# Selective scan on one core: GpSimd multiplies the scan results of two pairs by C in one instruction, and the first transfers of layer 2 go in another order

## What is computed

```python
def step(h, inp):
    x_t, dt_t, B_t, C_t = inp
    dA = jnp.exp(dt_t[:, :, None] * A)
    h = h * dA + (dt_t * x_t)[:, :, None] * B_t[:, None, :]
    y = jnp.einsum('bdn,bn->bd', h, C_t)
    return (h, y)
...
return ys.transpose(1, 0, 2) + x * D
```

## Time and profile before

| what | value |
|---|---|
| median of 3 runs | 19420.55 us (19398.34 to 19422.17) |
| profiled execution, its own time | 19405.06 us |
| its span from first to last instruction | 19403.3 us |
| VectorE busy | 17217.6 us (89%) |
| GpSimd busy | 16892.6 us (87%) |
| TensorE matmul busy | 15381.8 us (79%) |
| ScalarE busy | 13163.4 us (68%) |
| mean granted TensorE clock | 0.879 of full speed |
| DMA, mean rate | 94 GB/s |

### The profile page before, as it was taken

How to read it: one execution, slowest core, us unless ns; L and a number is a source line. 1 busy time by engine, 2 the same in 40 slices (tenths; PEclk the granted TensorE clock), 3 DMA queues, 4 the chain that set the end, 5 groups by cost and what they waited for, 6 DMA issues and landing times. The chain is left out here.

```text
span 19403.3 us, 188542 instructions
## 1 busy us (share of the span) xinstructions
PE 15381.8 (79%) x45152; PEld 5366.5 (28%) x45152; DVE 17217.6 (89%) x13583; ACT 13163.4 (68%) x33157; POOL 16892.6 (87%) x11028
## 2 busy tenths in 40 slices
PE   7887878878788787877878778787787877878778
PEld 2222222222222222222222222222222222222222
DVE  7988979889798897989979899798997989979899
ACT  5766767667676776767767677676776767767677
POOL 6979979799797997979979799797997979979799
PEclk8888888888898888888889888888888888888888
DMA  2424424244242442424424244242442424424244
GB/s 68 122 60 111 117 60 122 58 111 117 62 119 61 109 116 65 116 65 108 112 67 118 64 109 109 67 116 66 109 110 67 118 64 111 108 67 118 64 112 108
DMA packets 880283, 1820.18 MB, mean 94 GB/s; under 512 B 189530, under 2 KB 594804, under 8 KB 879028
## 3 DMA queue, kind: packets, MB, share of 16 engines
q1 hardware_dynamic: 879028, 1806.77, 37.0%
HBM read 1083.46 MB, written 245.63 MB: 68 GB/s over the span
## 5 line engine op out<-in xcount | busy, mean ns | idle before, releaser
L1156 DVE TENSOR_TENSOR_SCAN arena<-ps,arena 128x897 f32<-128x897 f32 x5376 | 10986.1, 2064 | 762.4 <-POOL arena L1351 292.7
L1359 POOL TENSOR_TENSOR arena<-arena 128x896 f32<-128x896 f32 x5376 | 9405.3, 1766 | 279.5 <-DVE arena L1156 259.6
L1290 ACT ACTIVATE ps<-arena,A 128x448 f32<-128x448 f32 x10752 | 6391.4, 627 | 2637.9 <-DVE arena L1156 2541.8
L1062 PE MATMUL ps<-arena,rep 128*64 128x448 f32 x21504 | 5477.2, 639 | 1626.5 <-POOL arena L1359 1618.2
L1351 POOL TENSOR_TENSOR arena<-arena 128x896 f32<-128x896 f32 x2688 | 4760.1, 1771 | 385.1 <-DMA arena<-arena 385.0
L1062 PEld LDWEIGHTS ps<-arena,rep 128*64 128x64 f32 x21504 | 1477.7, 153 | 5248.9 <-POOL arena L1359 2855.0
L1145 DVE TENSOR_TENSOR arena<-ps,arena 128x896 f32<-128x896 f32 x2688 | 2862.8, 1065 | 70.8 <-PE ps L982 60.0
L1015 PE MATMUL ps<-arena,diag 128*128 128x448 f32 x5248 | 2192.7, 562 | 75.4 <-DVE arena L1119 75.4
L1054 PE MATMUL ps<-arena,skipd 128*128 128x448 f32 x1344 | 802.6, 684 | 709.9 <-DVE arena L1132 590.0
L1015 PEld LDWEIGHTS ps<-arena,diag 128*128 128x128 f32 x5248 | 986.3, 195 | 1265.2 <-issue 1045.1
L1027 PE MATMUL ps<-arena,wdt 13*128 13x448 f32 x1344 | 764.9, 676 | 508.5 <-DVE arena L1125 496.9
(11 more groups left out here) (171 smaller groups left out, 18902.2 us busy)
## 6 DMA issues: line engine op xcount, KB each, us to landing
arena<-bc_rows SPq DMA_DIRECT2D x3584, 224.0 KB, 4.6
arena<-arena SPq DMA_DIRECT2D x4160, 112.0 KB, 3.2
x_projected<-arena SPq DMA_DIRECT2D x112, 672.0 KB, 3.6
y_forward<-arena SPq DMA_DIRECT2D x112, 672.0 KB, 5.3
arena<-x_projected SPq DMA_DIRECT2D x112, 672.0 KB, 4.8
arena<-y_forward SPq DMA_DIRECT2D x112, 672.0 KB, 6.2
x<-in_x SPq DMA_DIRECT2D x119, 336.0 KB, 3.6
x_normed<-arena SPq DMA_DIRECT2D x112, 336.0 KB, 5.2
```

The lines of the kernel that those rows point to most:

```text
L1062: m = e.matmul(ps[64 * h:64 * h + 64, YBANK, 0:T], rep[:, 0:64], pr[:, (q - 1 + h) % NPR, a * T:a * T + T], start=False, stop=p == NP - 1 ...
L1156: e.tensor_tensor_scan(rev(hh[:, q % NH, 0:W2], s), rev(decays(q)[:, 0:W2], s), rev(bb[:, q % NB, 0:W2], s), car[:, 2 * k + p % 2, n:n + 1 ...
L1290: e.activation(two(decays(q))[:, a, :], dt2[:, r % NR2, p % 2, :], ACT.Exp, scale=Am[s][:, 2 * k + p % 2, n:n + 1]).then_inc(c_ex, 1)
L1359: e.tensor_tensor(pr[:, q % NPR, :].rearrange("p (a b) -> p a b", a=2), two(hh[:, q % NH, :]), cr[:, p - p % 2:p - p % 2 + 2, :], ALU.mult ...
```

## The change

Three things are done together.

1. `output(q)` becomes `outputs(q)`: one GpSimd instruction of 1792 elements a partition handles pairs q and q+1. It waits for the scan of q+1 and for the sums of the two pairs that held its places in `pr`. `hh` gets 6 places.
2. GpSimd makes its product for pair g + 3 in step g, not g + 2, and `bb` gets 4 places.
3. The transfers of dt are split into two jobs (`dd`, `de`) with a semaphore each, so that a pair waits for the half that it reads. In the first pass of an image `ud` comes between the two, and the loads of B and C alternate. In later passes `ud` is due 0.6 steps earlier.

```diff
-NB, NH, NPR = 3, 3, 4
+NB, NH, NPR = 4, 6, 4
...
-        sp.extend([(max(t + 3.4, NP * (EJ * i + e - 2) - 0.5 if i else t), "dd", i, e), (t + 5, "ud", i, e)])
+        o = max(t + 3.4, NP * (EJ * i + e - 2) - 0.5 if i else t)
+        sp.extend([(o, "dd", i, e), (o + 0.02, "de", i, e), (t + 4.4 if i or e else o + 0.01, "ud", i, e)])
...
-            sp.append((max(r + 1, t + 2 + 4 * (G > 0 and not i)), "bl", i, G))
-            sp.append((max(r + 3, t + 2.1 + 4 * (not i)), "cl", i, G))
+            if i:
+                sp.extend([(max(r + 1, t + 2), "bl", i, G), (max(r + 3, t + 2.1), "cl", i, G)])
+            else:
+                sp.extend([(t + (5.3 if G else 2) + G, "bl", i, G), (t + 5.9 + G, "cl", i, G)])
...
         def decay(q):
             r, i, k, p, s = pair(q)
-            spread(w, s_dt, 4, r)
+            spread(w, s_dt, 2 * (r % NR2) + p % 2, r)
...
-        def output(q):
+        def outputs(q):
             r, i, k, p, s = pair(q)
-            w.wait_ge(c_sc, q + 1)
+            w.wait_ge(c_sc, q + 2)
             w.wait_ge(s_cl[p // 2], 32 * (i + 1))
-            w.wait_ge(c_sm, q - NPR + 1)
-            e.tensor_tensor(pr[:, q % NPR, :].rearrange("p (a b) -> p a b", a=2), two(hh[:, q % NH, :]),
-                            cr[:, p - p % 2:p - p % 2 + 2, :], ALU.mult).then_inc(c_mc, 1)
+            w.wait_ge(c_sm, q - NPR + 2)
+            o, h = pr[:, q % NPR:q % NPR + 2, :], hh[:, q % NH:q % NH + 2, :]
+            e.tensor_tensor(o.rearrange("p h (a b) -> p h a b", a=2),
+                            h.rearrange("p h (a b) -> p h a b", a=2)[:, :, :, 0:T],
+                            cr[:, p:p + 2, :].unsqueeze(1).to_broadcast([128, 2, 2, T]), ALU.mult).then_inc(c_mc, 2)
...
-        for g in range(-AHEAD, Q + 1):
-            if g >= 1:
-                output(g - 1)
-            if g + AHEAD < Q and not ON_VECTOR[(g + AHEAD) // NP % EJ][(g + AHEAD) % NP]:
-                product(g + AHEAD)
+        for g in range(-AHEAD - 1, Q + 1):
+            if g >= 2 and g % 2 == 0:
+                outputs(g - 2)
+            if g + AHEAD + 1 < Q and not ON_VECTOR[(g + AHEAD + 1) // NP % EJ][(g + AHEAD + 1) % NP]:
+                product(g + AHEAD + 1)
             side(g)
```

More of the change, by code:

```diff
@@ L905, in build @@
     s_xl, s_nl, s_yl = ([sem(f"{k}{b}") for b in range(2)] for k in ("xp_loaded", "n_loaded", "y_loaded"))
-    s_dt, s_du = ([sem(f"{k}{b}") for b in range(NR2)] for k in ("dt_spread", "du_spread"))
+    s_dt, s_du = ([sem(f"{k}{b}") for b in range(n)] for k, n in (("dt_spread", 2 * NR2), ("du_spread", NR2)))
     s_bl, s_cl = ([sem(f"{k}{G}") for G in range(4)] for k in ("b_loaded", "c_loaded"))
@@ L941, in b_loaded, with spread @@
         w.wait_ge(s_bl[p // 2], 32 * (i + 1))
-    def spread(w, sems, parts, r):
+    def spread(w, sems, k, r):
         if r >= 0:
-            w.wait_ge(sems[r % NR2], 16 * parts * (r // NR2 + 1))
+            w.wait_ge(sems[k], 32 * (r // NR2 + 1))
     def product_done(w, q):
@@ L1240, in side @@
                     o = ps[:, bank_of("t", i, k), 0:T]
-                    spread(w, s_dt, 4, r - NDT)
+                    for h in range(2):
+                        spread(w, s_dt, 2 * ((r - NDT) % NR2) + h, r - NDT)
                     w.wait_ge(c_du, r - NDT + 1)
@@ L1338, in side @@
                     w.wait_ge(c_dp, r - NDU + 1)
-                    spread(w, s_du, 2, r - NDU)
+                    spread(w, s_du, (r - NDU) % NR2, r - NDU)
                     e.tensor_tensor(du[:, r % NDU, :], dt[:, r % NDT, :], xc[:, r % NXC, :],
@@ L1347, in product @@
             r, i, k, p, s = pair(q)
-            spread(w, s_du, 2, r)
+            spread(w, s_du, r % NR2, r)
             b_loaded(w, i, p)
@@ L1420, in layer1_sync @@
                                     [64, 2, T])).then_inc(s_cl[k], 16)
-            if name == "dd":
+            if name in ("dd", "de"):
                 r = EJ * i + k
+                h = int(name == "de")
                 freed(w, "t", i, k)
                 w.wait_ge(c_ex, 2 * NP * (r - NR2 + 1))
-                for h in range(2):
-                    for j in range(2):
-                        e.dma_start(dt2[64 * j:64 * j + 64, r % NR2, h, :],
-                                    dt[64 * h:64 * h + 64, r % NDT, :]).then_inc(s_dt[r % NR2], 16)
+                for j in range(2):
+                    e.dma_start(dt2[64 * j:64 * j + 64, r % NR2, h, :],
+                                dt[64 * h:64 * h + 64, r % NDT, :]).then_inc(s_dt[2 * (r % NR2) + h], 16)
             if name == "ud":
```

## The result

The changed kernel takes 19911.17 us (19868.46 to 19934.89, 4 runs), the kernel before 19411.45 us beside it. The ratio is **1.0255**, 95% interval 1.0236 to 1.0274: 500 us slower, far outside the predicted range, on the side that had 9% of the chances. The profiled execution took 19868.46 us.

A forecast was written before the change was run, and what follows sets the result against it. VectorE's work plus its round trips over ScalarE and TensorE was taken as the bound, not GpSimd. Per image -15.7 + 2 + 4 + 1 - 3 = -11.7 us, times 16 images -187 us: 19225 us, range 18990 to 19325.

The forecast's parts named there:

- the side that had 9% of the chances: Whole kernel: slower than before by over 0.2%, given a chance of 0.09.
- The start, -15.7 +2 us an image: Start of layer 2: earlier dt x transfers bring the first scan 15.7 us forward; late first outputs give back 2 us.
- The merged instruction, 3.3 us: GpSimd's outputs: one merged instruction takes 3.3 us where two took 3.44, saving 24 us an image on GpSimd.
- Rival 1: Steady passes: GpSimd is the bound and the merge's saving is passed on, -33 us an image, 18890 us; chance 0.2.
- I count none of it: Steady passes: none of GpSimd's 24 us an image saved shortens the path, since VectorE does not wait for GpSimd.
- The second pass, +4 us: Second pass of an image: outputs 20, 21 and a dt x follow pair 24's late product, so scan 27 comes later.
- That order stays as it was: Second pass of an image: the queue's order is kept, so pair 24's product starts as late as before in its chain.
- places worth -3 us: Steady passes: more places in `hh` and `bb` and the earlier product remove VectorE's waits for GpSimd, -3 us an image.
- I count 0 for it, with 0.8 us a pass as the upper bound: Ends of groups: sums of y up to 1.6 us later behind merged outputs cost 0, at most 0.8 us a pass.
- The range: Whole kernel: -6 to -27 us an image, 18990 to 19325 us.
- -6 us an image: The range's slow end: start giving 13 us, second pass taking 5, steady passes taking 6; 19325 us.
- Rival 3: First chunk and group ends: late outputs hold ScalarE and TensorE, 0.8 us a pass, giving back the start; 19410 us; chance 0.1.

The follow-up runs named there:

- e1_start: The kernel before with only the third part of the change at the start (order of first transfers, half-dt semaphores), later `ud` as before; 19169.25 us, ratio 0.9867.
- e2_two: The changed kernel with each merged output written as two instructions, both behind the wait for the second scan; 20015.09 us, ratio 1.0304.
- e7_places: e1_start with four places in `bb` and six in `hh`, instruction order and single outputs as before; 19171.33 us, ratio 0.9877.
- e13_two_single: e3 with single outputs for pairs 10, 11 and 18, 19 of each forward pass, all others merged; 19402.19 us, ratio 0.9995.
- e18_start_norm_first: e1_start with the norm's matmul L992 ahead of the sum of pairs 18, 19 in TensorE's order; 19112.97 us, ratio 0.9852.
- e4_single: The changed kernel with one output instruction a pair again, each after its own scan; products stay a pair further ahead; 19518.28 us, ratio 1.0053.
- e3: The changed kernel with merged outputs, but products only as far ahead as in the kernel before; 19526.62 us, ratio 1.0052.
- e8: The changed kernel with only the first product of each group of pairs a step later, behind the next merged output; 19642.79 us, ratio 1.012.
- e10: e3 with six places for products with C and four for scan results; 19467.76 us, ratio 1.0019.
- e14: e3 with single outputs everywhere except pairs 10, 11 and 18, 19 of each forward pass, which stay merged; 19340.8 us, ratio 0.9968.
- e15: e3 with L1025 and L992 ahead of the sums of pairs 10, 11 and 18, 19 in TensorE's order; 19526.66 us, ratio 1.0065.
- e17: e3 with only L992 ahead of the sum of pairs 18, 19 in TensorE's order; 19460.67 us, ratio 1.0025.
- e11_backward: e3 with merged outputs in the backward passes alone, single ones in the forward passes; 19252.15 us, ratio 0.9909.
- e16_start_jobs_first: e1_start with L1025 and L992 ahead of the sums of pairs 10, 11 and 18, 19 in TensorE's order; 19442.32 us, ratio 1.0018.
- e9_lag_room: e3 with TensorE's sums one pair later, six places for products with C and four for scan results; 19961.44 us, ratio 1.0265.

## Why the prediction was wrong

- **The start, -15.7 +2 us an image.** Right within 1.3 us in the rows shown, and e1_start measured 16 us.
- **The merged instruction, 3.3 us.** Right, 3.31. Rival 1 fell: GpSimd was the busiest engine of a pass, but e2_two, which has 360 us more work on it than the changed kernel, is only 104 us (half a point) slower, where rival 1 needed the whole saving of 390 us to be passed on, 2 points. "I count none of it" was a little too strict. The Trainium skill says to optimise the engine with the highest occupancy first (Perfetto Trace Analysis, section Identifying the Most-Contended Engine); here that was GpSimd, and relieving it gave back under a third of its saved time.
- **The second pass, +4 us.** The delay came as worked out (16.0 us against 16.1), but its price did not: the lead lengthens the first two passes by 9.6 us with single outputs, and by 7.6 us with merged ones. How the delay grows on its way is not shown.
- **"That order stays as it was", and places worth -3 us.** This step failed. Places alone gave nothing (e7_places). The prediction priced the earlier product at the one pass where the trace of before already showed a wait for dt x. In the seven later passes where that wait was hidden by GpSimd's own work, with 1.2 us to spare in the pass shown, the lead took this cover away. Measured: 1.76 points, 21 us an image, where the sum had -3 + 4. Nearly half of it stands in the first two passes, the other half mostly in the passes with the new wait.
- **"I count 0 for it, with 0.8 us a pass as the upper bound".** This step failed by size. The 1.6 us of lateness was right and measured as 1.65. Its argument, that the convolution holds the sums anyway, was read at the ends of groups; what TensorE's order holds behind a sum in the middle of a group (L1025, L992) was not looked at. Measured: 1.85 points, 22 us an image, by the traces some 3.6 us in each of the four forward passes from the third on, and by the times 0.7 in a backward one.
- **The range.** Its slow end, -6 us an image, is not what its own bounds add up to: -13 + 2 + 5 + 1 + 6 is +1 us, about 19440 us. The result lies far above that too.
- **Rival 3** was this mechanism, at 0.8 us a pass and with a chance of 0.1. It should have had a bound of the full 1.6 us for each sum with something behind it, plus the slower matmuls.

The sum with measured terms: start -258, lead +340, merge +359 us, together +440 us of 500 measured. The remaining 60 us come where lead and merge are together: the lead costs 2.03 points with merged outputs and 1.76 with single ones. Which rows hold them is open.

## What to carry to other kernels

Before an instruction is put earlier in an engine's order, look at each place where its input comes late and is now covered by that engine's work, not only at those where a wait is to be seen: here a wait of zero had a margin of 1.2 us. Before two results are joined into one, go through the consumer's in-order list and ask of each job behind the consuming one who waits for it; the busy shares did not show this. And put the gains of a change on trial one by one: here a third of it was worth 1.3%, and the other two thirds cost 3.9%.

## What was not expected of the hardware

TensorE ran slower behind its waits: the same eight matmuls took 1.72 us at a granted clock of 1.00, 2.82 us at 0.59 behind a wait of 3.65 us, and 3.26 us at 0.50 behind one of 5.3 us. A late input so costs its own delay and up to 1.5 us more. The length of the last wait does not settle it: in e13_two_single they took 3.25 us at 0.52 behind one of 3.81 us, and 1.72 us at 1.00 behind one of 2.17 us.

Many forward passes came in one of two lengths. In two windows from about 450 us on they take 67.9 to 69.4 us in e1_start, e7_places, e18_start_norm_first and e4_single, and 71.3 to 71.8 us in the changed kernel and in e3, e8, e10, e13, e14, e15 and e17, at granted clocks from 0.81 to 0.90. Others fall outside: e11_backward has 67.9 and 70.7 us, e16_start_jobs_first 72.2 and 71.3, e2_two 74.8 and 71.7, e9_lag_room 78.4. Long ones are not those with the low clock alone (e13_two_single has 0.90), and what makes the step stays open.
